# Two-layer group-norm convolution: TensorE's waits for a unit placed in the unit ahead, and the intermediate's rows loaded as 48 + 48 partitions

## The reference

```python
def _gn(v, G=4, eps=1e-5):
    g = v.reshape(B_, G, C_ // G, H_, W_)
    m = jnp.mean(g, axis=(2, 3, 4), keepdims=True)
    s = jnp.var(g, axis=(2, 3, 4), keepdims=True)
    return ((g - m) / jnp.sqrt(s + eps)).reshape(v.shape)

x = x + _L0_conv_ref(_gn(x), L0_conv_weight, L0_conv_bias)
x = x + _L1_conv_ref(_gn(x), L1_conv_weight, L1_conv_bias)
```

## Time and profile before

| | us |
|---|---|
| three timed runs | 4224.03, 4220.69, 4217.2 (median 4220.69) |
| the profiled execution's own time | 4238.59 |
| its span, first to last instruction | 4236.8 |
| TensorE busy (matmul) | 3712.5, 88% |
| DVE / ScalarE / POOL busy | 2026.7 / 1763.8 / 1363.6 |
| mean granted TensorE clock | 0.978 |

### The profile page before, as it was taken

One profiled execution on the slowest core, in us unless ns is written; L12 is line 12 of the kernel. 1 busy time (PEld: TensorE's weight loads), 2 busy tenths in 40 slices (PEclk: granted clock), 3 DMA queues, 4 the chain that ended last, 5 costly groups with the idle time before them and its releaser, 6 DMA issues.

```text
span 4236.8 us, 87949 instructions
## 1 busy us (share of the span) xinstructions
PE 3712.5 (88%) x33232; PEld 1551.0 (37%) x33232; DVE 2026.7 (48%) x3110; ACT 1763.8 (42%) x1381; POOL 1363.6 (32%) x1829
## 2 busy tenths in 40 slices
PE   0087877898889999998889999999999999999999
PEld 0032322353333333353333333345564333343333
DVE  6866666565564444445556344444445222332222
ACT  0032222343334555533333555544443555555554
POOL 0011111111113545521111444441211555555555
PEclk9999898999999999999999999999999999999999
DMA  9989999999999999999999999999999999999997
GB/s 323 392 290 392 387 390 380 354 379 379 380 383 303 343 368 379 338 346 381 376 376 351 303 350 368 337 287 373 357 357 317 283 293 288 282 273 292 289 279 226
DMA packets 367108, 1435.02 MB, mean 339 GB/s; under 512 B 49888, under 2 KB 50016, under 8 KB 334176
## 3 DMA queue, kind: packets, MB, share of 16 engines
q10 hardware_dynamic: 176736, 627.30, 48.4%
q0 software_dynamic: 153344, 536.96, 33.5%
q1 hardware_dynamic: 36864, 268.45, 16.9%
HBM read 895.64 MB, written 536.87 MB: 338 GB/s over the span
## 4 chain that ended last, share of the span: by engine, by line
PE 56%; ACTq 12%; issue 12%; DMA 11%; DVE 6%; ACT 1%; POOL 1%; POOLq 0%; DVEq 0%; SPq 0%
PE conv L632 56%; ACTq L479 12%; DMA out_dram<-out_tile 8%; DMA stat_tile<-x_dram 2%; DVE bn_x L681 2%; ACT out_tile L465 1%; DVE out_tile L708 1%; DVE bn_mid L691 1%; POOL x_tile L405 1%; DMA mid_dram<-out_tile 1%; DVE mv_mid L719 1%; POOL out_dram L385 0%; DVEq L681 0%; DVE mv_x L713 0%; POOLq L385 0%
## 5 line engine op out<-in xcount | busy, mean ns | idle before, releaser
L632 PE MATMUL conv<-x_tile,wts 64*64 64x512 f32 x32832 | 3694.7, 600 | 281.2 <-ACT out_tile L465 190.0
L632 PEld LDWEIGHTS conv<-x_tile,wts 64*64 64x64 f32 x32832 | 1530.7, 135 | 2426.2 <-issue 2363.6
L465 ACT ACTIVATE out_tile<-conv,bias 128x1024 f32<-128x1024 f32 x688 | 729.1, 1111 | 1351.2 <-PE conv L632 749.6
L691 DVE BATCH_NORM_STATS2 bn_mid<-out_tile 128x512 f32 (+1 forms) x1376 | 849.5, 680 | 886.1 <-ACT out_tile L465 885.9
L708 DVE TENSOR_SCALAR out_tile<-conv,bias 128x1024 f32<-128x1024 f32 x340 | 436.4, 1283 | 1253.9 <-PE conv L632 1093.9
L371 POOL DMA_DIRECT2D mid_dram<-out_tile x680 | 344.7, 508 | 1712.2 <-ACT out_tile L465 1658.8
L470 ACT ACTIVATE out_tile<-conv,bias 128x1024 f32<-128x1024 f32 x344 | 383.5, 1115 | 831.9 <-PE conv L632 690.0
L508 ACT ACTIVATE x_tile<-x_tile 16x2048 f32<-16x2048 f32 x340 | 648.7, 1908 | 56.7 <-issue 37.4
L681 DVE BATCH_NORM_STATS2 bn_x<-stat_tile 128x512 f32 (+1 forms) x1024 | 629.1, 678 | 49.6 <-DMA stat_tile<-x_dram 49.4
L405 POOL COPY x_tile<-x_tile 16x2048 f32<-16x2048 f32 x340 | 639.8, 1882 | 1.6
L385 POOL DMA_DIRECT2D out_dram<-out_tile x680 | 349.9, 516 | 899.1 <-DVE out_tile L708 830.3
(11 more groups left out here) (62 smaller groups left out, 115.7 us busy)
## 6 DMA issues: line engine op xcount, KB each, us to landing
x_tile<-x_dram ACTq DMA_DIRECT2D x680, 512.0 KB, 22.7
stat_tile<-x_dram SPq DMA_DIRECT2D x256, 1024.0 KB, 9.9
out_dram<-out_tile POOLq DMA_DIRECT2D x680, 384.0 KB, 7.8
mid_dram<-out_tile POOLq DMA_DIRECT2D x672, 384.0 KB, 9.4
x_tile<-mid_dram ACTq DMA_DIRECT2D x340, 640.0 KB, 6.5
x_tile<-mid_dram ACTq DMA_DIRECT2D x344, 128.0 KB, 8.7
mid_dram<-out_tile POOLq DMA_DIRECT2D x8, 416.0 KB, 10.0
x_tile<-x_dram ACTq DMA_DIRECT2D x8, 256.0 KB
```

Source lines behind the costliest of these rows:

```text
L465: last = act.activation(out_tile[0:parts, slot, i], conv[0:parts, bank, i], ACT.Identity, bias=bias0[0:parts, win.parity, int(unit.last), ...
L632: last = nc.tensor.matmul(to, weights, x_tile[HALF * half:HALF * (half + 1), slot, middle, c + kw:c + kw + BANK], start=(kw == 0), stop=(k ...
L691: last = dve.bn_stats(bn_mid[0:parts, unit.win.pair % 2, i, bass.ds(unit.n * 2 + h, 1), :] .rearrange("p a b -> p (a b)"), out_tile[0:part ...
```

## The change

Three things. First, the rows of a layer-1 unit go to partitions 16 to 63 and 80 to 127, in two loads of 48 partitions, where there were one of 80 (16 to 95) and one of 16 (112 to 127). The lower half therefore has the same order of rows as the upper one, `PLACES` is one tuple, and both halo copies read and write other partitions (16 as before). Second, TensorE no longer has its waits at the start of a unit. The waits for unit n + 1 stand in unit n, in the second half of its columns: `wait_for_rows` ahead of kw = 0, `wait_for_halos` ahead of kw = 1, `wait_for_bank` ahead of kw = 2. Third, a layer-1 unit no longer waits for `x_loaded` on TensorE (the halo copies wait for it), except the last unit of the window. `load_mid` and `wait_for_mid` are the old functions moved outward; the loads stay on ScalarE's queue.

```diff
 BLOCKS0 = (((8, 0, 1), (16, 1, 2), (32, 5, 2), (48, 3, 2)),
-           ((0, 5, 2), (16, 1, 2), (32, 3, 2)),
+           ((0, 1, 2), (16, 5, 2), (32, 3, 2)),
...
-PLACES = ((0, 8, 16, 24, 48, 56, 32, 40), (32, 40, 16, 24, 48, 56, 0, 8))
+PLACES = (0, 8, 16, 24, 48, 56, 32, 40)
...
-MID_PARTS = 80
+BAND_PARTS = CH * ROWS_OUT
...
                 pool.tensor_copy(x_tile[0:PAIR, unit.slot, :, 1:SIDE + 1],
-                                 x_tile[HALF:HALF + PAIR, earlier.slot, :, 1:SIDE + 1]) \
+                                 x_tile[HALF + 2 * PAIR:HALF + 3 * PAIR, earlier.slot, :,
+                                        1:SIDE + 1]) \
...
-                load_rows(VALID, first, MID_PARTS, x_loaded[slot])
-                load_rows(P - PAIR, first + MID_PARTS, PAIR, x_loaded[slot])
+                load_mid(act, unit, PAIR, first, BAND_PARTS, x_loaded[slot])
+                load_mid(act, unit, HALF + PAIR, first + BAND_PARTS, BAND_PARTS, x_loaded[slot])
...
-                act.activation(x_tile[HALF + HALF // 2:HALF + HALF // 2 + PAIR, unit.slot, :,
-                                      1:SIDE + 1],
-                               x_tile[HALF // 2:HALF // 2 + PAIR, unit.slot, :, 1:SIDE + 1],
+                act.activation(x_tile[HALF:HALF + PAIR, unit.slot, :, 1:SIDE + 1],
+                               x_tile[2 * PAIR:3 * PAIR, unit.slot, :, 1:SIDE + 1],
...
+            def wait_for_rows(unit):
+
+                if unit.win.layer == 0 or unit.last:
+                    pe.wait_ge(x_loaded[unit.slot], (unit.turn + 1) * 32)
+                if unit.win.layer == 1 and unit.kind == TOP:
+                    pe.wait_ge(edge_loaded, 16 * (same_layer_before(unit.win) + 1))
+                if isinstance(unit.n, int) and unit.n < X_RING:
+                    pe.wait_ge(pads_written, unit.win.w * X_RING + unit.n + 1)
+                pe.sem_inc(unit_begun)
+
+            def wait_for_halos(unit):
+
+                if unit.win.layer == 1 and unit.kind != TOP:
+                    pe.wait_ge(first_halo, halos_through(unit))
+                if unit.win.layer == 1 and not unit.last:
+                    pe.wait_ge(second_halo, halos_through(unit) + 1)
+                pe.sem_inc(unit_begun)
+
+            def wait_for_bank(unit):
+
+                earlier = unit.before(2)
+                if earlier is None:
+                    return
                 pe.wait_ge(evicted_a, earlier.count + 1)
                 if earlier.win.layer == 1:
                     pe.wait_ge(evicted_v, earlier.layer_count + 1)
+                pe.sem_inc(unit_begun)
...
                     for kw in range(KW):
+                        if c and following is not None:
+                            if kw == 0:
+                                wait_for_rows(following)
+                            elif kw == 1:
+                                wait_for_halos(following)
+                            else:
+                                wait_for_bank(following)
```

More of the change, by code:

```diff
@@ L256, in halos_through, with load_mid, wait_for_mid @@
             return same_layer_before(unit.win) * UNITS + unit.n
+        def load_mid(queue, unit, part, first, rows, done):
+            both = mid[unit.win.image:unit.win.image + 2, bass.ds(first, rows), :]
+            queue.dma_start(x_tile[part:part + rows, unit.slot, :, 1:SIDE + 1],
+                            both.rearrange("n r w -> r n w")).then_inc(done, 16)
+        def wait_for_mid(queue, win):
+            done = next(v.w for v in WINDOWS if v.layer == 0 and v.pair == win.pair) + 1
+            for s in range(RING):
+                queue.wait_ge(stored[s], 32 * len(range(s, done * UNITS, RING)))
+            queue.wait_ge(stored_last, 16 * last_stores(done))
         AGGREGATE, MEAN, VAR, ROOT, WEIGHTS = (TAIL + X_RING + d for d in (0, 4, 5, 6, 7))
@@ L326, in _ @@
                         ident1[half, VALID + row - 1:VALID + CH * ROWS_OUT:ROWS_OUT],
-                        one[half, 0:CH], [[-1, CH]], ALU.is_equal, 0.0, -PLACES[i][row], 1))
+                        one[half, 0:CH], [[-1, CH]], ALU.is_equal, 0.0, -PLACES[row], 1))
             alone(pool.affine_select(own_group[:, 0, 0], one[:, 0:BOTH], [[-2 * ROWS_IN, BOTH]],
@@ L446, in _ @@
                     if r in TAKEN_IN[kind]:
-                        place = HALF * i + PLACES[i][r]
+                        place = HALF * i + PLACES[r]
                         act.dma_start(rows1[place:place + CH, kind, :, CH * lo:CH * hi],
@@ L488, in load @@
                     return
[L490 to L493, removed]
                 first = unit.n * OUT_ROWS + CH
                 if unit.last:
-                    load_rows(PAIR, first, PAIR, x_loaded[slot])
-                    load_rows(3 * PAIR, first + PAIR, CH, x_loaded[slot])
+                    load_mid(act, unit, PAIR, first, PAIR, x_loaded[slot])
+                    load_mid(act, unit, 3 * PAIR, first + PAIR, CH, x_loaded[slot])
                     return
                 if unit.kind == TOP:
-                    load_rows(CH, 0, CH, edge_loaded)
-                load_rows(VALID, first, MID_PARTS, x_loaded[slot])
-                load_rows(P - PAIR, first + MID_PARTS, PAIR, x_loaded[slot])
+                    load_mid(act, unit, CH, 0, CH, edge_loaded)
+                load_mid(act, unit, PAIR, first, BAND_PARTS, x_loaded[slot])
+                load_mid(act, unit, HALF + PAIR, first + BAND_PARTS, BAND_PARTS, x_loaded[slot])
             def copy_second_halo(unit):
                 act.wait_ge(x_loaded[unit.slot], (unit.turn + 1) * 32)
-                act.activation(x_tile[HALF + HALF // 2:HALF + HALF // 2 + PAIR, unit.slot, :,
-                                      1:SIDE + 1],
-                               x_tile[HALF // 2:HALF // 2 + PAIR, unit.slot, :, 1:SIDE + 1],
+                act.activation(x_tile[HALF:HALF + PAIR, unit.slot, :, 1:SIDE + 1],
+                               x_tile[2 * PAIR:3 * PAIR, unit.slot, :, 1:SIDE + 1],
                                ACT.Identity).then_inc(second_halo, 1)
[L513 to L518, removed]
             def take_root(n):
@@ L536, in step @@
                         if following.b == 0 and following.win.layer == 1:
-                            wait_for_mid(following.win)
+                            wait_for_mid(act, following.win)
                         neighbour = unit.after(1)
-                        if win.layer == 1 and neighbour is not None and neighbour.win is win:
+                        if win.layer == 1 and neighbour is not None \
+                                and neighbour.win is win:
                             act.wait_ge(first_halo, halos_through(neighbour))
@@ L596, in bias_sum @@
                 last.then_inc(bias_summed, 1)
-            def wait_for_bank(earlier):
+            def wait_for_rows(unit):
[16 more added lines that the diff above has]
+                    return
                 pe.wait_ge(evicted_a, earlier.count + 1)
@@ L601, in wait_for_bank @@
                     pe.wait_ge(evicted_v, earlier.layer_count + 1)
+                pe.sem_inc(unit_begun)
             def convolve(unit, read=None):
                 win, slot, bank = unit.win, unit.slot, unit.bank
[L605 to L615, removed]
+                following = unit.after(1)
                 for c in range(0, SIDE, BANK):
@@ L643, in _ @@
             bias_sum(0, 0)
+            wait_for_rows(Unit(WINDOWS[0], 0))
             for win in WINDOWS:
@@ L647, in step @@
                 def step(unit, in_loop):
-                    earlier = unit.before(2)
-                    if earlier is not None:
-                        wait_for_bank(earlier)
                     read = None
```

## The result

The changed kernel takes 4868.61 us (median of 4 runs, 4861.25 to 4875.76) against 4220.41 us before; the ratio is 1.1535, 95% interval 1.1514 to 1.1557. It is slower by 15.4%. Its profiled execution took 4861.25 us, with a span of 4859.5 us, 622.7 us more than the earlier trace rows.

The account below looks back on a forecast made before the run. It took TensorE's matmul pace, 5.15 us a unit, as the bound, with 148 us of second-layer pauses. 4238.6 + 593 (halo wait) + 80 (clock) = 4912 us, set to 4895 against the timed median; range 4790 to 5080.

Parts of the forecast that it names:

- The halo wait in series with POOL's copy: Second layer: TensorE stops at the moved wait every unit, 8 matmuls joining the copy's chain; +593 us.
- The period of a unit: Second layer: eviction to eviction takes 7.36 us in loop units and 7.16 us in straight-line units.
- The first unit of a window: Second-layer windows: counted among the 28 straight-line units, at 7.16 us.
- The loop's exit: Second-layer windows: POOL's copy is late once a window, and that unit takes 10.43 us.
- The clock: Second-layer loops: idle gaps of 1.98 us may lower TensorE's clock; +80 us, between 0 and 374.
- Rival A: Second layer: every loop unit falls to the low clock, 374 us, total 5188 us; chance 0.1.
- First-layer windows: TensorE's earlier bank and rows waits there cost 0, at most 56 us.
- Rival B: First-layer windows: late stops grow by 0.86 us x 65, total 4951 us; chance 0.12.
- rival D: Moved waits do nothing, each taking place where the unit boundary's was; 4221 us; chance 0.02.
- The loads: Second-layer row loads of 48 + 48 partitions cost 0; the split needs 38% more packet time to decide anything.
- Rival E: Second layer: split loads set a new bound, 8.0 us a unit at 50% more packet time, 5101 us; chance 0.03.
- rival C: Second layer: waits are met early, perhaps hidden by TensorE's 64-instruction queue; pauses vanish, 148 us faster, 4073 us; chance 0.03.

Follow-up runs that it names:

- e3: Changed kernel with only the halo wait put back at the start of its own unit: 4205.44 us, ratio 0.9977 to the kernel before.
- e2: Changed kernel's moved waits alone, with the 80 + 16 partition loads and `PLACES` of the kernel before: 4880.71 us, ratio 1.1572 to the kernel before.
- e9: Changed kernel with the halo wait four matmuls earlier, ahead of kw = 0, 12 matmuls behind it: 5519.09 us, ratio 1.3072 to the kernel before.
- e4: Changed kernel with the halo wait four matmuls later, ahead of kw = 2 beside the bank wait: 4614.25 us, ratio 1.0948 to the kernel before.
- e5: Changed kernel with POOL's first-halo copy ahead of its stores, still behind its wait for the evictions: 4291.83 us, ratio 1.0130 to the kernel before.
- e6: Changed kernel with POOL's first-halo copy ahead of its stores and its wait for the evictions: 4204.29 us, ratio 0.9928 to the kernel before.
- e1: Changed kernel's 48 + 48 layout alone, with TensorE's waits at the unit's start as before: 4218.75 us, ratio 0.9996 to the kernel before.
- e7: e6 plus ScalarE's second-halo copy ahead of its eviction, all TensorE waits in the unit ahead: 4171.97 us, ratio 0.9853 to the kernel before.
- e8: e7 with all of TensorE's waits back at the unit's start: 4164.83 us, ratio 0.9844 to the kernel before.
- e11: Same kernel as e8, run again in more rounds: 4148.49 us, ratio 0.9828 to the kernel before.

## Why the prediction was right, point by point

**The halo wait in series with POOL's copy: right, and shown.** The wait list has the 604.9 us and 339 waits that were forecast as 600 to 700 us and about 340. e3 and e2 show that this wait alone does it; e9 and e4 that each matmul put behind it costs 0.215 us a unit; e5 that an earlier copy takes most of the loss away, and e6 that the same wait is harmless once the copy is early enough.

**The period of a unit: right mechanism, resumption mis-sized.** Forecast 7.36 us in the loops and 7.16 outside. In the last window's loop it was 7.25: the copy ended at A + 5.09 where the earlier trace rows had A + 5.14, and TensorE resumed 0.15 us later and not 0.21. In the other three loops the resumption was 0.24 us, and the 173 loop units that didn't fall took 7.34 us on average: 4 us less than forecast in all, in part because two errors cancelled. Outside the loops the copy's end was exact (A + 4.79) and the resumption 0.15 us and not the 0.36 of the earlier trace rows. The prediction took that figure from a place with five waits and used it at a place with two. 6.94 us is the result; with a fifth of these units at 7.2 to 7.3 us their mean is 7.0, which makes 17 us less than forecast. The 8 matmuls and 0.29 us were exact.

**The first unit of a window.** The sum had it as one of the 28 straight-line units, at 7.16 us. In it stands the wait for the halo of the window's second unit, which POOL copies behind the evictions and stores of the last unit of the window ahead, and from that unit's eviction to its own it takes 9.60, 8.22, 8.23 and 8.12 us: 6 us more than forecast in all. The loop's exit took 11.1 to 12.0 us instead of 10.43, 5 us more in all.

**The clock: right in kind, about right in size.** Forecast 80 us between bounds of 0 and 374. The granted clock was 0.96 to 0.97 in the second-layer windows, which by an estimate from these two numbers is 0.035 of 2559 us or 90 us of array work lost; 54 us of longer units can be read in the loops (in four of these POOL's copy itself was late by 1.3 us). Counted from the mean of 7.34 they are 49 us, and two straight-line units that fell add 5. Of the lost work a bit more than half lay on the chain, and half is what the prediction took. The half was a choice between two bounds, so that it came so near is in part luck. Rival A, every loop unit falling, didn't happen: the gaps of the changed kernel lie on both sides of 1.94 us, where falling began, and above it 42 rows of 111 fell. e9 shows that at 2.7 to 2.9 us nearly all do. The Trainium skill (TensorE: Matmul & The Clock Gate, HAM oscillation) describes bursts that each begin at the low clock; by e9 this is what four of five loop units do here, by the changed kernel it is one of five, and the straight-line units with gaps of 1.55 us never do.

**First-layer windows: right.** 0 forecast, 14 us less measured in one execution of each; the experiments scatter by as much (e1 has 512 us and e3 500 for the same window), so nothing is read into it. Rival B is out, and rival D (no change) with the result.

**The loads: right in time.** e1 puts the layout at 0.9996. Rival E is out: the packets' time grew by about an eighth, against the 38% that it took to decide anything. The forecast of a DMA share near 0.75 was too low for the same reason: 0.80 to 0.93, where e2 with the old loads has 0.71 in the last window.

**The queue of TensorE (rival C's argument).** In the timeline of the changed kernel TensorE stops inside the unit (4501.93 to 4503.63), so a queue of instructions doesn't carry the matmuls past a wait: the order decides, as the Trainium skill's page (TensorE: Matmul & The Clock Gate) has it for matmuls. Rival C's condition, a halo ready before A + 3, was made true in e6 and e7, and the kernel did become faster then, though by 0.7 to 1.5% and not by 148 us (3.5%), and for both copies together the copies did it, not the waits: e8 and e11 have it without them.

**Sum.** 593 + 80 = 673 us forecast, 622.7 us measured between the profiled executions, 50 too much. The terms: clock 26 too much, straight-line units 17, first-layer windows 14 and loop units 4, against 6 too little for the first units and 5 for the exits. That makes 50. The median came out at 4869 us for 4895. That this is only 26 us off and not 50 is luck: the profiled execution of the kernel before was 18 us above its median and that of the changed kernel 7 below its own.

## What to carry to other kernels

A wait that moves to an earlier place in an engine's list is free only if what it waits for is done by then; measure the time from the event that starts the producer to its end (here A + 5.1), and compare it with the time at which the consumer gets to the new place (A + 3.1). If it's later, everything between the new place and the old one joins the producer's chain, and in a loop where the consumer starts the producer again that sum is the new period. The better move was at the other end: a copy that needs nothing of the current unit was put ahead of the wait and the stores that it stood behind, and this made the kernel 1.5 to 1.7% faster with the consumer's waits in either place.

## What the runs showed of the hardware that wasn't expected

How fast TensorE resumes after a wait isn't one number. From the end of POOL's copy to the first matmul it took, in straight-line code, 0.15 us where the place has the two halo waits alone (the changed kernel, e2, e9), 0.30 us with the two waits for the bank behind them (e4), and 0.31 to 0.37 us with the five waits of the kernel before. In the loops it was 0.15 us in the last window and 0.24 in the other three with the halo waits alone, 0.21 us in the last two windows and 0.35 in the first two with the waits of the kernel before, and 0.49 us in all four in e4. So what stands at the place counts, but the same source lines gave different times in different windows, and no run here shows why.

The clock depends on the length of a regular gap, and the step is narrow. Behind POOL's copy in the changed kernel none of 175 rows fell at gaps of up to 1.93 us and 42 of 111 fell at 1.94 to 2.25 us; e2 repeats it with none of 172 and 37 of 108. In e9, at 2.7 to 3.0 us, 160 of 174 fell, at 1.7 us each. The gap alone doesn't settle it: in e9, behind units that had just run at the low clock, gaps of 2.0 to 2.4 us cost nothing in 19 of 19.
